# Merged mask products, split gates and halved output transfers in a two-layer attention and expert kernel

## The reference

```
x = x + attention0(layernorm(x), ctx, ctx)          # 16 heads of 8, context of 64 tokens
x = x + moe0(layernorm(x))                          # 8 experts, top 2 by sigmoid gate, + shared
x = x + block1(layernorm(x), ctx)                   # causal attention over itself, then attention
                                                    # over ctx, layernorms and a dense layer
x = x + moe1(layernorm(x))                          # top 1 of 8 (7 real experts), + shared expert
```

## Time and profile before

| | us |
|---|---|
| median of 3 runs | 335.74 |
| lowest and highest run | 334.33, 340.63 |
| the profiled execution's time | 338.23 |
| its span, from the first to the last instruction | 336.1 |
| second attention, first product to last unit | about 117 to 199 |
| gate of group 0, first DVE instruction | 243.33 |
| gate of group 1, first DVE instruction | 286.34 |
| last matmul's end | 332.1 |

### The profile page before, as it was taken

The page is one execution under the profiler, slowest core; times in us unless marked ns, Lnnn a source line. Parts: engine busy times, 40 slices in busy tenths (PEclk is TensorE's granted clock), DMA queues, the critical chain, the costliest instruction groups (busy, mean ns, idle before and its releaser), DMA issues.

```text
span 336.1 us, 8921 instructions
## 1 busy us (share of the span) xinstructions
PE 291.7 (87%) x3475; PEld 222.8 (66%) x3475; DVE 257.9 (77%) x694; ACT 209.6 (62%) x442; POOL 152.2 (45%) x157
## 2 busy tenths in 40 slices
PE   5787957599999998989998999775898999999994
PEld 5655746455656645777776787544655999759993
DVE  4699977874664897977999577789689996894832
ACT  3665973445469649777867999234763648745561
POOL 9902898546344111443434345312431666432551
PEclk9999976958999999997999999799699999999998
DMA  7600223522400000000000000000002202040211
GB/s 249 252 2 1 97 96 100 180 98 91 137 0 2 0 0 4 2 2 2 2 2 3 2 2 3 2 0 0 3 3 108 82 4 97 2 168 21 90 41 32
DMA packets 6609, 16.64 MB, mean 50 GB/s; under 512 B 676, under 2 KB 2984, under 8 KB 6568
## 3 DMA queue, kind: packets, MB, share of 16 engines
q1 hardware_dynamic: 6568, 16.08, 13.6%
HBM read 10.83 MB, written 0.52 MB: 34 GB/s over the span
## 4 chain that ended last, share of the span: by engine, by line
PE 52%; DVE 31%; ACT 5%; POOL 4%; issue 4%; DMA 1%; SPq 0%; DVEq 0%; ACTq 0%
PE ps L808 8%; PE ps L810 7%; PE ps L809 7%; DVE MX L1400 6%; PE ps L1037 5%; DVE prl L667 3%; DVE stat L1355 2%; POOL prl L667 2%; PE ps L869 2%; PE ps L1129 2%; PE ps L870 2%; PE ps L881 2%; PE ps L1025 2%; PE ps L1099 2%; DVE pr L1576 2%
## 5 line engine op out<-in xcount | busy, mean ns | idle before, releaser
L667 POOL TENSOR_TENSOR prl<-pr,prh 128x384 f16<-128x384 f32 (+1 forms) x48 | 49.4, 1029 | 76.0 <-ACT pr L1188 76.0
L1185 ACT ACTIVATE prh<-ps 128x384 f16<-128x384 f32 (+1 forms) x96 | 51.2, 534 | 17.6 <-PE ps L810 6.6
L1400 DVE TENSOR_REDUCE MX<-ps 128x8 f32<-128x512 f32 (+2 forms) x80 | 52.1, 682 | 8.3 <-PE ps L911 4.5
L672 POOL TENSOR_TENSOR prl<-pr,prh 128x512 f16<-128x512 f32 x28 | 32.7, 1171 | 43.6 <-ACT prh L1225 43.6
L777 POOL TENSOR_TENSOR wl<-wraw,wh 128x512 f16<-128x512 f32 (+1 forms) x30 | 33.5, 1137 | 18.1 <-DVE wh L1288 18.0
L667 DVE TENSOR_TENSOR prl<-ps,prh 128x384 f16<-128x384 f32 (+1 forms) x48 | 28.5, 594 | 6.3 <-ACT ps L1188 5.9
L1576 DVE TENSOR_TENSOR pr<-ps,hr 128x512 f32<-128x512 f32 x28 | 19.0, 685 | 11.9 <-ACT hr L1219 10.7
L819 PE MATMUL ps<-cst 128*128 128x128 f32 x120 | 21.9, 321 | 4.7 <-DMA cst<-in_const 4.1
L1188 ACT ACTIVATE ps<-ps 128x384 f32<-128x384 f32 (+1 forms) x48 | 25.8, 538 | 0.0
L1188 ACT ACTIVATE pr<-ps 128x384 f32<-128x384 f32 (+1 forms) x48 | 25.6, 533 | 0.0
L1219 ACT ACTIVATE hr<-ps 128x512 f32<-128x512 f32 x28 | 16.5, 597 | 13.6 <-PE ps L810 12.8
(11 more groups left out here) (256 smaller groups left out, 1045.2 us busy)
## 6 DMA issues: line engine op xcount, KB each, us to landing
wraw<-in_weights SPq DMA_DIRECT2D x8, 768.0 KB, 4.0
wraw<-wh SPq DMA_DIRECT2D x6, 384.0 KB, 2.6
wraw<-wl SPq DMA_DIRECT2D x6, 384.0 KB, 3.0
wraw<-in_weights SPq DMA_DIRECT2D x2, 576.0 KB, 7.3
rowb<-in_rows SPq DMA_DIRECT2D x1, 708.0 KB, 4.6
wd<-in_down SPq DMA_DIRECT2D x1, 576.0 KB, 7.3
X<-in_x SPq DMA_DIRECT2D x2, 256.0 KB, 4.0
picks<-in_spread SPq DMA_DIRECT2D x1, 512.0 KB, 5.0
```

The source lines that it names most:

```text
L667: return engine.tensor_tensor(prl[:, g, three, 0:width], whole, prh[:, g, three, 0:width], ALU.subtract)
L672: return engine.tensor_tensor(hlo[:, g, k % NPV, :], hh[:, g, k % 2, :], hhi[:, g, k % NPV, :], ALU.subtract)
L1185: nc.scalar.activation(high, src[:, 0:width], ACT.Exp, scale=SCALE[a]).then_inc(pr_ready, 1)
L1400: nc.vector.tensor_reduce(o, src[:].rearrange("p (h k) -> p h k", h=heads), AX_X, ALU.max).then_inc(max_read, 1)
```

## The change

Five edits.

1. **Mask products of attention 1.** `MT` gets 128 more columns per sequence, a second copy of the transposed maxima of its last 128 queries. With it, one product of 384 columns replaces those of 256 and 128, and the two products of the triangle become one of 256 columns over both diagonal blocks.
2. **The transposition of the maxima** makes that copy: a third product of 128 columns on PE, and the cast by ACT has 384 columns.
3. **Gate and rank** of the last layer become five events: `gate1` (PE, DVE up to the difference, ACT's exponential), `prob1`, `pick1`, `rank` up to the last reading of PSUM, `rank_end`. Each is a separate part for the planner, so that other DVE work can stand between them. `rank`'s PSUM bank is free after `rank` and no longer after the whole.
4. **The planner** gets new durations for these, edges (`gate1` of group 0 after `gate0` of group 1, that of group 1 after `rank_end` of group 0), the urgencies of the old kinds for the new ones, and `patience`: an event with patience counts as if it could start that much sooner, so its engine is kept for it. ACT has 3.0 us for the exponential, DVE 0.5 us for the four later events of group 1.
5. **Output.** The last addition signals after two of four tiles (`pair_added`), and each group's output is two transfers of 128 KB.

```diff
 def experts1(g, normed, turned):
-        gate = chain([("gate1", g), ("rank", g)], turned)
+        gate = chain([("gate1", g), ("prob1", g), ("pick1", g), ("rank", g), ("rank_end", g)], turned, ("gate0", 1),
+                     *[("rank_end", 0)] * g)
...
-            "lo1": [("pool", 1.17)], "xsplit": [("act", .6), ("pool", 1.2)], "rank": [("pe", .5), ("dve", 2.6)],
+            "lo1": [("pool", 1.17)], "xsplit": [("act", .6), ("pool", 1.2)], "rank": [("pe", .5), ("dve", 1.5)],
...
-            "gate0": [("pe", 1.), ("dve", 4.0)], "gate1": [("pe", .9), ("dve", 3.5)],
+            "gate0": [("pe", 1.), ("dve", 4.0)], "gate1": [("pe", .6), ("dve", .5), ("act", .25)], "prob1": [("dve", .65)], "pick1": [("dve", 1.9)],
+            "rank_end": [("dve", 1.3)],
...
+    def patience(e, s):
+
+        if e[0] == "gate1":
+            return 3.0 if s == 2 else 0.0
+        return PATIENCE if e[0] in ("prob1", "pick1", "rank", "rank_end") and e[1] else 0.0
...
-                starts.append((t + (TABLE_LOAD if engine == "act" and other_table(e) else 0.0), e, s))
+                t += TABLE_LOAD if engine == "act" and other_table(e) else 0.0
+                starts.append((t - patience(e, s), e, s))
         soonest = min(starts)[0]
         t, e, s = max((x for x in starts if x[0] <= soonest), key=lambda x: urgency(x[1]))
+        t += patience(e, s)
...
-        if e[0] in ("gate0", "gate1") and engine == "dve":
+        if e[0] == "gate0" and engine == "dve":
...
-        MT = sb("MT", [P, B, S], BF16)
+        MT = sb("MT", [P, B, S + P], BF16)
...
             for g in range(G):
-                sp.wait_ge(add_read, nth[("add1", g, 1)])
-                sp.dma_start(out.rearrange("(g t p) d -> p g t d", g=G, p=P)[:, g], X[:, g]).then_inc(out_done, 16)
-            sp.wait_ge(out_done, 16 * G)
+                for i in range(2):
+                    sp.wait_ge(*((add_read, nth[("add1", g, 1)]) if i else (pair_added, g + 1)))
+                    tt = slice(2 * i, 2 * i + 2)
+                    sp.dma_start(out.rearrange("(g t p) d -> p g t d", g=G, p=P)[:, g, tt], X[:, g, tt]).then_inc(out_done, 16)
+            sp.wait_ge(out_done, 32 * G)
...
-                    for t in range(2):
-                        mm = nc.tensor.matmul(o[:, t * P:(t + 1) * P], MP[:, e[2], t, :], identb[:], start=True, stop=True)
+                    for i, t in enumerate((0, 1, 1) if e[1] == 1 else (0, 1)):
+                        mm = nc.tensor.matmul(o[:, i * P:(i + 1) * P], MP[:, e[2], t, :], identb[:], start=True, stop=True)
...
-                        nc.tensor.matmul(o[:, 0:S], headsel[:, u:u + 1].broadcast_to([P, P]), mt, **kw)
-                        nc.tensor.matmul(o[:, S:S + P], headsel[:, u:u + 1].broadcast_to([P, P]), mt[:, P:S], **kw)
-                        for c in (0, S):
-                            mm = nc.tensor.matmul(o[:, c:c + P], identb[:], trib[:, 1, :], **kw)
+                        nc.tensor.matmul(o[:, 0:S + P], headsel[:, u:u + 1].broadcast_to([P, P]), mt, **kw)
+                        mm = nc.tensor.matmul(o[:].rearrange("p (c k) -> p c k", k=S)[:, :, 0:P], identb[:],
+                                              trib[:, 1, :].unsqueeze(1).broadcast_to([P, 2, P]), **kw)
...
-                    take(bank[e][0], pos_ready, n)
+                    take(bank[e][0], ranked, n)
...
-                nc.scalar.copy(MT[:, e[2], :], src[:, 0:S]).then_inc(negT_ready, 1)
+                    width = S + P if e[1] == 1 else S
+                    nc.scalar.copy(MT[:, e[2], 0:width], src[:, 0:width]).then_inc(negT_ready, 1)
...
                     nc.vector.tensor_tensor(zz[:], logits, r1[:].broadcast_to([P, T, 8]), ALU.subtract).then_inc(g1_sub, 1)
-                    dve.wait_ge(g1_exp, n)
+                elif kind == "prob1":
+                    dve.wait_ge(g1_exp, nth[("gate1", e[1])])
...
+                elif kind == "pick1":
+                    g = e[1]
...
-                    link(nc.vector.tensor_tensor(zz[:], zz[:], before, ALU.add))
+                    nc.vector.tensor_tensor(zz[:], zz[:], before, ALU.add).then_inc(ranked, 1)
+                    dve.wait_ge(ranked, n)
+                elif kind == "rank_end":
+                    g = e[1]
...
+                            if t == 1:
+                                ins.then_inc(pair_added, 1)
```

More of the change, by code:

```diff
@@ L54 @@
 ARRIVES = {"ctx": 4.5, "masks0": 5., "masks1": 5., "bias": 7., ("split", 0): 5.5, "split": 14.0, ("ln_stats", "x0"): 7.0, "bo_add": 10.0, "kbs_zero": 8.5}
-PRESSING = {'add0': 254, 'add1': -540, 'b3_add': -131, 'back': 243, 'bias': 172, 'bias_split': -413, 'bo_add': 366, 'ctx': -274, 'down0': 129, 'down1': -341, 'downr': 1630, 'gate0': -306, 'gate1': 767, 'hi1': 268, 'kblocks': 1032, 'kbs_zero': -623, 'ln_center': 4, 'ln_norm': -107, 'ln_plain': 862, 'ln_pow': 667, 'ln_stats': 644, 'lo1': 991, 'masks0': -184, 'masks1': 38, 'max': 160, 'nat': 679, 'negmax': 1540, 'onehot': 522, 'onehot_t': -718, 'out_norm': 873, 'plow': 928, 'plow_pool': -487, 'pv': 539, 'rank': 1369, 'scores': 158, 'sort_high': -349, 'sort_low': 692, 'spill': 356, 'split': 158, 'split_low': -1854, 'spots': -295, 'spread': 1018, 'square': 1246, 'stack': 173, 'turn': 727, 'up0': 128, 'up1': -352, 'v1': 615, 'vctx': 308, 'xsplit': -982}
+PRESSING = {'add0': 254, 'add1': -540, 'b3_add': -131, 'back': 243, 'bias': 172, 'bias_split': -413, 'bo_add': 366, 'ctx': -274, 'down0': 129, 'down1': -341, 'downr': 1630, 'gate0': -306, 'gate1': 767, 'prob1': 767, 'pick1': 767, 'rank_end': 1369, 'hi1': 268, 'kblocks': 1032, 'kbs_zero': -623, 'ln_center': 4, 'ln_norm': -107, 'ln_plain': 862, 'ln_pow': 667, 'ln_stats': 644, 'lo1': 991, 'masks0': -184, 'masks1': 38, 'max': 160, 'nat': 679, 'negmax': 1540, 'onehot': 522, 'onehot_t': -718, 'out_norm': 873, 'plow': 928, 'plow_pool': -487, 'pv': 539, 'rank': 1369, 'scores': 158, 'sort_high': -349, 'sort_low': 692, 'spill': 356, 'split': 158, 'split_low': -1854, 'spots': -295, 'spread': 1018, 'square': 1246, 'stack': 173, 'turn': 727, 'up0': 128, 'up1': -352, 'v1': 615, 'vctx': 308, 'xsplit': -982}
+PATIENCE = 0.5
 SHARED = 6
@@ L272, in group @@
         return e[2] // 2
-    if e[0] in ("gate0", "gate1", "spread", "up0", "up1", "hi1", "lo1", "down0", "down1", "add0", "add1", "bo_add", "b3_add",
+    if e[0] in ("gate0", "gate1", "prob1", "pick1", "rank_end", "spread", "up0", "up1", "hi1", "lo1", "down0", "down1", "add0", "add1", "bo_add", "b3_add",
                 "xsplit", "rank", "onehot", "sort_high", "sort_low", "spots", "onehot_t", "downr", "back", "spill"):
@@ L604, in build @@
         spread_split, spread_mm, spread_ready = sem("spread_split"), sem("spread_mm"), sem("spread_ready")
-        add_read = sem("add_read")
+        add_read, pair_added = sem("add_read"), sem("pair_added")
         in_slots, in_spill = sem("in_slots"), [sem("in_spill0"), sem("in_spill1")]
@@ L1079, in _ @@
                     pe.wait_ge(routing_ready, 2)
-                    pe.wait_ge(sel_ready, n)
-                    take(bank[e][0], pos_ready, n)
+                    pe.wait_ge(sel_ready, nth[("pick1", g)])
+                    take(bank[e][0], ranked, n)
                     one = onecol[:, 0:1].broadcast_to([P, P])
@@ L1102, in _ @@
                 elif kind == "spots":
-                    pe.wait_ge(pos_ready, nth[("rank", e[1])])
+                    pe.wait_ge(pos_ready, nth[("rank_end", e[1])])
                     take(bank[e][0], spots_ready, n)
```

4 lines of the change are left out of this document (2 added, 2 removed).

## The result

| | before | after |
|---|---|---|
| median, us | 335.3 (4 runs, 334.33 to 340.63) | 341.96 (4 runs, 338.09 to 343.4) |
| profiled execution: time, span | 338.23, 336.1 | 338.09, 336.3 |
| group 0's gate, first DVE instruction | 243.3 | 240.3 |
| from there to the end of the span | 92.8 | 96.0 |

The ratio of the times is 1.0153, with a 95% interval of 1.0079 to 1.0226: the changed kernel is slower by 0.8 to 2.3%. The forecast was 334.4 us, a ratio just under 1. (Before has one run more here than in the 335.74 us above.) A second comparison of the same kernel, with 12 runs against 29, gave 1.0143 (1.0086 to 1.0199), medians 340.97 and 336.77.

The account below looks back on a forecast made before the run. PE was taken as the bound, its last 90 us nearly without holes. Masks -0.2, transposition +0.2, gates -1.0 and output -0.3 summed to -1.3 us, from 335.74 to 334.4 us; range 331.5 to 338.1.

Parts of the forecast that it names:

- the gates' -1.0 in the sum: Gates and ranks in five events: other DVE work at the seams partly closes PE's holes, -1.0 us, ends -4.9 and +2.8.
- The forecast's own sign for it: Group 0's gate to first sorting product, 11.3 us before: under 10.7 supports holes closing, over 12.7 a slower kernel.
- the doubling of 4 columns: Gates' doubling of the top probability, 161 or 1,125 ns beside POOL: each gate can win or lose 964 ns by shifting.
- `rank`'s bank: The rank's PSUM bank comes free four small instructions earlier; no PE wait was put down to the rank's end: 0.
- Rival D: Pieces slip into group 0's seams, one-hot 2.8 us late, PE out of shared-expert work: 336.3 to 339 us, chance 0.16.
- F: Order's tail turns out badly: routed experts meshed otherwise, PE running dry, clock at 1.2 GHz; 339 to 345 us, chance 0.05.
- The masks: Second attention's 64 units: four matmuls instead of six over the same 1,024 columns, -0.2 us, ends 0 and -0.8.
- rival E: The 128 fewer weight loads count after all, 12.4 us: time 323.3 us, chance 0.02.
- The cast of 384 columns: Maxima's transposition: ACT's wider cast near 0.50 us, first block exposed in full; +0.2 us with the third product, ends 0 and +0.7.
- The count of matmuls: Sign in the profile after: PE's matmuls fall by 124 but for fillers.
- The order ahead of the gates: No shift expected before the gates; wrong if windows before 240 us shift by more than 1 us.
- The output: Group 1's output in two transfers, the last moving 128 KB instead of 256: -0.3 us, ends -0.6 and +0.1.

Follow-up runs that it names:

- the gates alone: The kernel before with only gates and ranks cut into events and the planner's patience (edits 3 and 4): ratio 1.0107 to before, 96.1 us from gate to end.
- the kernel with both last edits: Changed kernel, two transposed one-hot tiles behind a routed copy and POOL's first two group 1 subtractions cut to 64 columns: ratio 0.9962 to before.
- the masks alone: The kernel before with only the mask products and the transposition changed (edits 1 and 2), order as before: ratio 1.0007 to before.
- the output alone: The kernel before with only the output in two transfers for each group (edit 5): ratio 0.9997 to before, 92.6 us from gate to end.

## Why the prediction was wrong

**The step that failed is the gates' -1.0 in the sum.** Measured is +3.2 us from gate to end, and 1.1% with the gates alone. The mechanism that the step assumed, holes of PE closed by pieces put at the seams, did not take place: PE's time without a product grew from 4.26 to 7.86 us. The forecast's own sign for it, the distance from gate to first sorting product, did not move either: 11.2 us where it was 11.3, neither under 10.7 nor over 12.7. The step looked for gain and harm between the gate and the one-hot. Both losses lie elsewhere: in group 0 some 30 us behind the one-hot, in group 1 right at it.

Three of its premises were wrong.
- It took what lies behind the gates as fixed, and added what the holes around them give. The planner, though, decides all that follows anew. PE's order is the same for its first 402 of 495 events, DVE's differs at once behind the gate, and two of the new neighbourhoods are bad ones.
- It priced the meeting of DVE and POOL with one row, the doubling of 4 columns, 161 and 1,125 ns, as 0 in the sum and +-1 in the range. The wide 16-bit instructions pay it too, and they are the ones that PE waits for (below). In the small ones the shift did take place: in group 0's rank an instruction on 128 x 8 elements (`jump`) took 1.05 us beside POOL before and 0.17 after, so what the rank won there (0.88) the one-hot matrix lost (0.90).
- It put `rank`'s bank at 0. PE now waits 0.6 us for it, although the edit frees it earlier within the rank. The 0 holds for the end all the same: the kernel with both last edits has this wait too (0.6 us), and is at 92.9 us from gate to end.

The trace of before had shown the second point on the instruction that mattered. The four one-hot instructions of group 0 and of group 1, before (count; duration in ns, min/median/max; first and last start):

```profile
L1528 DVE TENSOR_SCALAR route<-copies,pos x4: 543/546/547, 252.6 to 254.0; 128x1280 f16<-128x1280 f16 x4
...
L1528 DVE TENSOR_SCALAR route<-copies,pos x4: 540/540/1248, 297.0 to 299.1; 128x1280 f16<-128x1280 f16 x4
```

and after:

```profile
L1547 DVE TENSOR_SCALAR route<-copies,pos x4: 541/546/1444, 248.6 to 250.9; 128x1280 f16<-128x1280 f16 x4
...
L1547 DVE TENSOR_SCALAR route<-copies,pos x4: 542/992/1447, 295.7 to 298.9; 128x1280 f16<-128x1280 f16 x4
```

An instruction of 0.54 us takes 1.25 to 1.45 where POOL is at work: 0.7 to 0.9 us for each meeting. Before, it happened once in the two groups; after, once in group 0 and twice in group 1. With this row the bound for the gates' step could have been put at 0.9 us upward for each new meeting. At the two places three are new (both tiles, and one more of group 1's one-hot instructions than before): 2.7 us, an estimate, where 3.2 were measured.

**Rival D had the right side and the wrong mechanism.** Its price, +2.8 us, is close to the +3.2 from gate to end, but the one-hot matrix of group 0 was not late. One piece did slip into a seam there (`out_norm`, between `rank` and `rank_end`), but it had stood ahead of the one-hot before, too; the rank ended earlier (7.7 us after the gate, 8.5 before, when the multiplication stood ahead of it), and moving the multiplication back changed nothing. Group 0's one-hot did take 2.83 us instead of 1.93 and ended no later. **F** named "meshed otherwise" and PE running dry, which is what happened, but with the clock at the lower level, which did not: it is 1.00 in all four windows after. The median, 341.96, lies in F's interval and outside of the range of 331.5 to 338.1. Of its size the trace shows 3.2 us. The ratios, 1.0153 and 1.0143, are 5.1 and 4.8 us, with intervals from 2.6 to 7.6 and from 2.9 to 6.7; 3.2 lies in both. Whether the part ahead of the gate adds something is open: its orders are the same, and executions of one order differ there by more.

**What held.**
- The masks: -0.2 was forecast, and the masks with the transposition measured 1.0007 (+-0.5%). A unit's four products take 0.43 us, from 188.50 to the next product behind them at 188.93 (timeline of after), where 0.43 to 0.44 was forecast:

```profile
188.50 0.27 PE L974 MATMUL ps<-QS,kbs 128*128 128x256 f16 x1
188.60 0.22 PE L975 MATMUL ps<-QS,kbs 128*128 128x128 f16 x1
188.66 0.33 PE L976 MATMUL ps<-MT,headsel 128*128 128x384 bf16 x1
188.82 0.27 PE L977 MATMUL ps<-trib,identb 128*128 128x256 bf16 x1
188.93 0.27 PE L924 MATMUL ps<-KBX,QS 128*128 128x256 f16 x1
```

- Weight loads (rival E): 132 of them are gone and PEld is busy 4.4 us less. With the masks alone 124 are gone, and no time came of it, 1.0007. E's 12.4 us are excluded. The Trainium skill, Perfetto Trace Analysis, section Identifying the Most-Contended Engine, advises the busy share of weight loads, beside the share of the peak rate, to judge how near the limit TensorE works; it does not promise time for loads taken away, and here none is seen for them (to half a per cent).
- The cast of 384 columns: 487 ns in the mean, 0.50 for the first, as forecast from the earlier trace rows. The exposure that was costed in full for the first block didn't show: PE is without a product for 0.61 us there, where it was 0.66. The reading behind it was wrong, since the product (L882) starts at 125.72, just before the cast's end at 125.76 (timeline of after):

```profile
124.92 0.69 DVE L1332 TENSOR_TENSOR tL<-ps,tH 128x512 f16<-128x512 f32 x1 [0.24 <-ACT tH L1170]
125.26 0.50 ACT L1188 CAST MT<-ps 128x384 bf16<-128x384 f32 x1
125.72 0.38 PE L882 MATMUL ps<-tH,picks 128*128 128x512 f16 x1 [0.61 <-issue]
```

  It starts 0.11 us after the end of DVE's subtraction `tL` (125.61), and before the change 0.10 us after it (128.83 and 128.93), so that subtraction, and not the cast, is likely what PE waited for; no run tests it.
- The count of matmuls: 124 fewer but for fillers, as forecast.
- The order ahead of the gates did not shift. The sign given for it, windows before 240 us within 1 us, was a bad one: the gate falls 3.0 us earlier in this execution, with the same orders, as it does between executions of the kernels with single edits.
- The output: -0.3 was forecast. From the last addition's end to the end of the span it is 2.74 us before, 2.55 with the output alone and 2.62 after, so 0.1 to 0.2 us. The step read the wrong size: the 2.8 us of the earlier trace rows are the median of two transfers, 3.4 for group 0's and 2.3 for group 1's, and only the second stands at the end. Its 2.3 us became 2.1 to 2.2 for each half in these two kernels. The issues:

```profile
332.55 1.13 DVE L1608 SCALAR_TENSOR_TENSOR X<-ps,wtop,X 128x128 f32<-128x128 f32 x4 [0.79 <-PE ps L1141]
333.18 1.25 SPq L739 DMA_DIRECT2D out<-X  x2
```

The 1.25 us are from the start of the first issue to the end of the second (0.37 and 0.73 us), with SP's wait for the last addition between them: the second starts at 333.7, when that addition is done (333.68), so SP wasn't late.

The Trainium skill, DMA: Bandwidth & Descriptors, section Anatomy of one DMA, gives some 2 us of a transfer as fixed, for those that GpSimd issues, and counts the rest by size at 436 GB/s. Estimated from that page, 128 KB less would save 0.3 us, and not the 0.15 that the prediction drew from it; measured are 0.1 to 0.2, and no run shows the fixed part by itself.

## What to carry to other kernels

Splitting an event for a list scheduler is not a local edit: price it by comparing the two orders on each engine up to the first difference, and then by looking behind that difference for instructions that PE waits for, not by adding up the holes near the split. Where the plan has no term for two engines that slow each other, look for the lines whose durations spread widely (here 0.54 to 1.45 us for one line), and treat every place in which such an instruction, on PE's path, meets the other engine as a cost of its own, read off that spread. To separate the code from the order, run the new code in the old order first; and in a kernel whose start varies, measure from a mark behind the varying part.

## What the runs showed of the hardware

- DVE beside POOL: the same four instructions of 128 x 1280 16-bit elements took 1.94 us with POOL idle, 2.04 beside two POOL instructions of 0.5 us, 2.63 where one of 1.16 us met them, and 3.73 beside two of these, which themselves took 2.70 instead of 2.32. Both engines lose. Not every DVE instruction does: the shared multiplication, 128 x 512 in float32 with one input from PSUM, took 0.66 to 0.69 us in all 28 cases before and after, among them one that ran wholly beside a POOL subtraction (at 259.53 us of after). The Trainium skill, SBUF — State Buffer, section SBUF: two separate sides, describes this as an exclusive lock on a pair of ports that one engine holds for a whole instruction. The rows agree with that in kind and size (an added 0.7 to 0.9 us, no more than one POOL instruction of 1.16).
- The time before the gate: with the same orders, the gate of group 0 fell anywhere from 237.3 to 245.9 us, and mostly the later the lower the mean granted clock of the execution (0.965 at 237.3, 0.938 at 245.9). A straight line through the span against the mean clock of 167 executions of all these kernels falls by 2.6 us for each 0.01 of clock. The kernel before alone had runs from 332 to 341 us, with clocks from 0.965 to 0.937. What sets the clock apart between executions is open.
- The issue of one output transfer of group 1 took SP 0.39 us for 256 KB; with two of 128 KB the first took 0.37 and the second 0.37 to 0.82 us. The landings came 2.0 to 2.3 us after the start of each issue.
